# Layer 0's scores moved from its edge stage into the stage that spreads the edges

## The reference, cut to what matters

```python
h = x @ W_w + W_b                       # 6250 x 128
row, col = (edge_index[0], edge_index[1])
a_src, a_dst = (a_w[:DIM], a_w[DIM:])
e = h[row] @ a_src + h[col] @ a_dst + a_b
e = leaky_relu(e, negative_slope=0.01)
attention = softmax(e, axis=0)
msg = attention * h[col]
out = segment_sum(msg, row, num_segments=N_NODES)
```

## Time and profile before

| | |
|---|---|
| median of 3 runs | 11,844.06 us (11,843.0 to 11,853.68) |
| span of the profiled execution, first to last instruction | 10,283.7 us |
| what lies around the span (median less span) | 1,560.4 us |
| spread stage, from SP's first load to the end of GpSimd's last scatter | 520 to 2,764 us |
| edge stage of layer 0, up to the first instruction of the next stage | 2,764 to 3,785 us |

### The profile page before, as it was taken

One profiled execution on the slowest core, in us unless ns is written; L12 is line 12 of the kernel. 1 busy time (PEld: TensorE's weight loads), 2 busy tenths in 40 slices (PEclk: granted clock), 3 DMA queues, 4 the chain that ended last, 5 costly groups with the idle time before them and its releaser, 6 DMA issues. The chain is left out here.

```text
span 10283.7 us, 161996 instructions
## 1 busy us (share of the span) xinstructions
PE 6978.8 (68%) x46439; PEld 5971.3 (58%) x46440; DVE 6132.2 (60%) x14585; ACT 2692.4 (26%) x4442; POOL 5216.0 (51%) x5267
## 2 busy tenths in 40 slices
PE   3543334443377757778877763999984888888885
PEld 2243333333377655666666652666654888888885
DVE  8832222222277776666666654777776666666665
ACT  5022222222255562222222212444441000000000
POOL 0067777777500007777777752000003777777773
PEclk7766666666688878999999986999996666666665
DMA  4055454545544435555555571000002333333335
GB/s 167 13 154 156 157 157 156 157 155 158 154 122 121 120 97 158 148 149 152 152 154 152 155 124 54 0 0 0 0 1 64 104 103 106 106 104 103 104 108 82
DMA packets 1150548, 1137.43 MB, mean 111 GB/s; under 512 B 239363, under 2 KB 959825, under 8 KB 1150117
## 3 DMA queue, kind: packets, MB, share of 16 engines
q1 hardware_dynamic: 948422, 666.82, 23.0%
q0 software_dynamic: 195904, 465.66, 16.7%
q10 hardware_dynamic: 6048, 2.84, 0.1%
HBM read 731.30 MB, written 403.51 MB: 110 GB/s over the span
## 5 line engine op out<-in xcount | busy, mean ns | idle before, releaser
L1051 POOL DMA_INDIRECT buf<-node_rows,buf x1728 | 1745.0, 1010 | 527.5 <-issue 526.3
L1563 POOL DMA_INDIRECT buf<-node_rows_ln,buf x1728 | 1715.5, 993 | 563.4 <-issue 498.0
L717 POOL DMA_INDIRECT edge_rows_by_src<-buf x1728 | 1692.6, 980 | 550.8 <-issue 526.1
L1081 PE MATMUL psum<-buf 128*128 128x128 f32 x1728 | 368.9, 369 | 1306.2 <-DVE buf L1044 1306.2
L1081 PEld LDWEIGHTS psum<-buf 128*128 128x128 f32 x1728 | 300.0, 197 | 1326.6 <-issue 1326.6
L2066 PE MATMUL psum<-parts,buf 128*128 x4896 | 917.2, 329 | 99.5 <-DVE buf L2102 44.8
L809 DVE COPY buf<-buf 128x32 int32<-128x32 int32 x108 | 19.9, 185 | 1469.5 <-DMA buf<-records_by_dst 1469.3
L2044 ACT CAST buf<-psum 128x1024 bf16<-128x1024 f32 x612 | 619.2, 1012 | 693.0 <-PE psum L2055 693.0
L2082 DVE TENSOR_TENSOR buf<-buf,ends_of 128x2048 bf16<-128x2048 bf16 x616 | 727.0, 1222 | 111.5 <-issue 111.5
L2447 PE MATMUL psum<-buf 128*128 128x5 f32 x3456 | 747.9, 354 | 49.3 <-ACT buf L2424 49.3
L2447 PEld LDWEIGHTS psum<-buf 128*128 128x128 f32 x3456 | 738.3, 329 | 63.3 <-ACT buf L2424 63.3
(11 more groups left out here) (431 smaller groups left out, 14202.6 us busy)
## 6 DMA issues: line engine op xcount, KB each, us to landing
buf<-edge_rows_by_src SPq DMA_DIRECT2D x114, 1056.0 KB
buf<-edge_rows_by_src SPq DMA_DIRECT2D x110, 1024.0 KB
buf<-in_edge_attr SPq DMA_DIRECT2D x864, 128.0 KB
running_weighted_sums<-buf SPq DMA_DIRECT2D x108, 544.0 KB, 3.5
buf<-loc_rows_by_src SPq DMA_DIRECT2D x110, 512.0 KB, 5.1
buf<-loc_rows_by_dst SPq DMA_DIRECT2D x110, 512.0 KB, 4.6
running_sums<-buf SPq DMA_DIRECT2D x108, 512.0 KB
edge_rows_by_src<-buf SPq DMA_DIRECT2D x139, 260.0 KB, 2.8
```

Of the source, the lines that this page charges most:

```text
L717: nc.gpsimd.indirect_dma_start(rows, bass.IndirectOffsetOnAxis(ap=at[:, h, t:t + 1], axis=0), st[:, h, t, :], None).then_inc(scattered[h], 16)
L1051: nc.gpsimd.indirect_dma_start(rows[:, t, 0:used], None, table, bass.IndirectOffsetOnAxis(ap=stage[:, t:t + 1], axis=0)).then_inc(sem, 16)
L1081: last = nc.tensor.transpose(psT[:, sg % 2, t * P:(t + 1) * P], oh[:, 4 * sg + t, :], c["ident"][:])
L1563: nc.gpsimd.indirect_dma_start(xn[:, j, t, :], None, table1, bass.IndirectOffsetOnAxis(ap=stage[:, j // 4, at:at + 1], axis=0)).then_inc(g ...
```

## The change

The scores of layer 0 are found in the spread stage. For each half VectorE there compares two sets of one-hots in bf16 (by destination and by source, `sel`), TensorE turns both, and ScalarE copies both out of PSUM. The source's one-hots are multiplied with the three bf16 parts of the source scores of all 49 blocks at once (`find`, 48 matmuls of 49 columns), and VectorE picks each edge's own block out of the 49 columns (`of_blk`, `picked`), adds the destination's part and the bias, takes the leaky relu and writes the score into the column of the row that held the destination's part. It also keeps a maximum of the scores, which is spread to all partitions after the last half (`negm`). VectorE's order becomes: the places of half n+1, then the scores of half n. GpSimd's wait for `evacuated` goes; `placed` is now given after the score is written.

The edge stage of layer 0 goes half by half. ScalarE takes the exponent with the final maximum, VectorE makes each weighted one-hot with a single instruction per tile (compare and multiply, L1267 of the new kernel), TensorE sums and VectorE adds (L1278). Turned one-hots, the running maximum, the factor and the scaling of `agg` are gone.

```diff
             c["agg"] = agg
-            l0_edges(nc, c, ins, blk_a, a_parts, rows)
+            l0_edges(nc, c, blk_a, negm, rows)
...
                         pool.wait_ge(edge_got[h], 128 * i + 128)
-                        pool.wait_ge(evacuated, 4 * n + 6)
...
+                def keep_dst(n, g):
+                    act.wait_ge(dst_turned, 2 * n + (g + 5))
+                    act.wait_ge(expanded, 8 * n + (4 * g + 4))
+                    nc.scalar.copy(dstT[:, g, :], psT[:, 0, :]).then_inc(dst_kept, 1)
+
+                def keep_src(n, g):
+                    act.wait_ge(src_turned, 2 * n + (g + 5))
+                    act.wait_ge(scored, 2 * n + (g + 1))
+                    nc.scalar.copy(srcT[:, g, :], psT[:, 1, :]).then_inc(src_kept, 1)
+
+                def evacuate(n, h, x):
+                    act.wait_ge(expanded, 8 * n + (x + 9))
+                    nc.scalar.copy(st[:, h, 2 * x:2 * x + 2, D:D + WT], psX[:, x % 2, 0:2 * WT].rearrange("p (t k) -> p t k", t=2)).then_inc(evacuated, 1)
...
-                        evacuate(n, h, 3)
+                        keep_dst(n, 0)
+                        keep_src(n, 0)
+                        keep_dst(n, 1)
+                        for x in range(4):
+                            evacuate(n, h, x)
+                        keep_src(n, 1)
+                        for x in range(4, 8):
+                            evacuate(n, h, x)
                 for g in range(QC):
                     act.wait_ge(loc_turned, g + 1)
...
+                        def turn(w, g, turned):
+                            for t in range(G):
+                                tile = G * g + t
+                                last = nc.tensor.transpose(psT[:, w, t * P:(t + 1) * P], sel[:, h % 2, w, tile // 2, :, tile % 2], ident[:])
+                            last.then_inc(turned, 1)
+
+                        def expand(x):
+                            pe.wait_ge(evacuated, 8 * n + (x + 1))
+                            for t in range(2):
+                                tile = 2 * x + t
+                                last = nc.tensor.matmul(psX[:, x % 2, t * WT:(t + 1) * WT], dstT[:, tile // G, (tile % G) * P:(tile % G + 1) * P],
+                                                        flat(tab[:, bass.ds(blocks[x], 1), 0:WT]), start=True, stop=True)
                             last.then_inc(expanded, 1)

+                        def find(g):
+                            pe.wait_ge(src_kept, 2 * n + (g + 2))
+                            for t in range(G):
+                                for k in range(3):
+                                    last = nc.tensor.matmul(psS[:, g, t * NB:(t + 1) * NB], srcT[:, g, t * P:(t + 1) * P], parts[:, k, :], start=(k == 0), stop=(k == 2))
+                            last.then_inc(scored, 1)
...
                         pe.wait_ge(hot, n + 1)
-                        for g in range(4):
-                            pe.wait_ge(ohT_ready, 4 * n + (g + 1))
-                            turn_onehot(nc, c, oh[:, h % 2], psT, g).then_inc(turned, 1)
-                            if g:
-                                expand(g - 1)
-                        expand(3)
+                        pe.wait_ge(dst_kept, 2 * n + 1)
+                        turn(0, 0, dst_turned)
+                        pe.wait_ge(src_kept, 2 * n + 1)
+                        turn(1, 0, src_turned)
+                        pe.wait_ge(dst_kept, 2 * n + 2)
+                        turn(0, 1, dst_turned)
+                        for x in range(4):
+                            expand(x)
+                        pe.wait_ge(src_kept, 2 * n + 2)
+                        turn(1, 1, src_turned)
+                        pe.wait_ge(chosen, n + 1)
+                        find(0)
+                        pe.wait_ge(dst_kept, 2 * n + 3)
+                        for x in range(4, 8):
+                            expand(x)
+                        find(1)
...
+                    lp.link(nc.vector.tensor_scalar(locs[:, b, 0, :], place[:], -1.0, None, ALU.add))
+                    dve.wait_ge(dst_turned, 2 * n + 2)
+                    dve.wait_ge(src_turned, 2 * n + 2)
+                    for w in range(2):
+                        last = nc.vector.tensor_tensor(sel[:, b, w], bc(iota[:].unsqueeze(1), [P, PAIRS, P, 2]),
+                                                       bc(locs[:, b, w, :].rearrange("p (a t) -> p a t", t=2).unsqueeze(2), [P, PAIRS, P, 2]), ALU.is_equal)
+                    last.then_inc(hot, 1)
+                    lp.link(nc.vector.tensor_copy(node[:], field(1)))
+                    lp.link(nc.vector.tensor_tensor(key[:], node[:], field(2).bitcast(F32), ALU.subtract))
+                    lp.link(nc.vector.tensor_tensor(of_blk[:, b], blk_no[:], bc(key[:].unsqueeze(1), [P, NB, HALF]), ALU.is_equal))
+                    lp.link(nc.vector.tensor_scalar(lost[:, b], valid[:], -1.0, -NEG, ALU.add, ALU.mult))
...
+                    of_dst = st[:, h, :, SCORE:SCORE + 1].rearrange("p t o -> p (t o)")
+                    dve.wait_ge(scored, 2 * n + 4)
+                    lp.link(nc.vector.tensor_tensor(picked[:].rearrange("p (g t) k -> p g t k", g=2), psS[:, :, 0:G * NB].rearrange("p g (t k) -> p g t k", t=G),
+                                                    of_blk[:, b].rearrange("p k (g t) -> p g t k", g=2), ALU.mult))
+                    dve.sem_inc(chosen, 1)
+                    lp.link(nc.vector.tensor_reduce(score[:], picked[:], AX.X, ALU.add))
+                    dve.wait_ge(evacuated, 8 * n + 10)
+                    lp.link(nc.vector.scalar_tensor_tensor(score[:], score[:], ab[:], of_dst, ALU.add, ALU.add))
+                    lp.link(nc.vector.scalar_tensor_tensor(of_dst, score[:], 0.01, score[:], ALU.mult, ALU.max))
+                    dve.sem_inc(placed, 1)
+                    lp.link(nc.vector.tensor_tensor(cand[:], of_dst, lost[:, b], ALU.add))
+                    lp.link(nc.vector.tensor_tensor(most[:], most[:], cand[:], ALU.max))
...
+                def step(i, h):
+                    n = R * i + h
+                    if not isinstance(i, int) or n + 1 < NH:
+                        find_places(n + 1, (h + 1) % R, i if h + 1 < R else i + 1)
...
+                        find_scores(n, h, 1 if isinstance(i, int) and n == NH - 1 else 2)
...
+                dve.wait_ge(max_spread, 1)
+                nc.vector.tensor_scalar(negm, psM[:, P:P + 1], -1.0, None, ALU.mult)
...
+    agg, R = c["agg"], 4
+    assert NH % R == 0 and NT + R * HALF <= NTX
...
+                    sp.dma_start(rows[:, s], by_tile[:, s * HALF:(s + 1) * HALF, D:ROW]).then_inc(got[s], 16)
+                with sp.Fori(0, NI) as i:
+                    for s in range(R):
+                        sp.wait_ge(summed, R * i + (s + 1))
+                        sp.wait_ge(saved, R * i + (s + 1))
+                        sp.dma_start(rows[:, s], by_tile[:, bass.ds(i * (R * HALF) + (s + R) * HALF, HALF), D:ROW]).then_inc(got[s], 16)
...
+                    for s in range(R):
+                        n = R * i + s
+                        act.wait_ge(got[s], 16 * i + 16)
+                        act.wait_ge(weighed, n + 1)
+                        nc.scalar.activation(p[:, s % 2, :], rows[:, s, :, D + 1:D + 2].rearrange("p t o -> p (t o)"), ACT.Exp, bias=negm).then_inc(weights, 1)
+                        tiles = bass.ds(i * (R * HALF) + s * HALF, HALF)
...
+                    for s in range(R):
+                        n = R * i + s
+                        pe.wait_ge(weighed, n + 3)
+                        pe.wait_ge(added, PAIRS * n + 1)
+                        for q in range(PAIRS):
+                            for k in range(2):
+                                t = 2 * q + k
+                                last = nc.tensor.matmul(psA[:, s % 2, q // 3, (q % 3) * W:(q % 3) * W + D + 1], oh[:, s % 2, t, :], rows[:, s, t, 0:D + 1],
+                                                        start=(k == 0), stop=(k == 1))
+                            if q == 2:
+                                last.then_inc(partly, 1)
                         last.then_inc(summed, 1)
...
+                def weigh(n, s, i):
+                    dve.wait_ge(weights, n + 1)
+                    if not isinstance(n, int) or n >= 2:
+                        dve.wait_ge(summed, n - 1)
+                    for t in range(HALF):
+                        last = nc.vector.tensor_scalar(oh[:, s % 2, t, :], c["iota"][:], rows[:, s, t, W - 2:W - 1], p[:, s % 2, t:t + 1], ALU.is_equal, ALU.mult)
+                    last.then_inc(weighed, 1)
+
+                def add(n, s, i):
+                    blocks = pair_blocks(nc, ENG.DVE, blk, i, s, 0, R)
+                    dve.wait_ge(partly, n + 1)
...
+                        if q == 3:
+                            dve.wait_ge(summed, n + 1)
+                        dve.wait_ge(added, PAIRS * n + (PAIRS + q + 1))
```

(20 more changed lines are left out.)

378 lines of the change are left out of this document (108 added, 270 removed).

## The result

In the comparison that the prediction was made for, the changed kernel took 12,058.28 us (median of 4 runs, 12,046.06 to 12,060.26) and the kernel before, in runs made beside it, 11,848.87 (4 runs): ratio 1.0174 [1.0152, 1.0196]. The medians are 209 us apart, slower, where 168 us less were forecast.

What follows compares the result with a forecast made beforehand. Prediction: GpSimd's scatters bound the spread stage and VectorE the edge stage; -241 (edge) + 66 (contention) + 7 (start) = -168, so 11,844 - 168 = 11,676 us, range 11,580 to 11,795.

Steps and rivals of the forecast that it cites:

- 1,560.4 us lie around the span and are carried over unchanged: Whole kernel: profile span 10,283.7 us against a timed median of 11,844.06; the difference was taken as time outside the span.
- It waits for nothing else: Spread stage: GpSimd's scatters wait only for issue, so a half costs 20.6 us and 108 halves 2,220 us.
- Rival (c): Spread stage: TensorE–ScalarE hand-overs and `find` gating `placed` make a half 23.3 us, total 11,903 us, slower; chance 0.08.
- Edge stage: Edge stage of layer 0: 7.05 us a half, 761 us for 108, ending at 3,544 against 3,784.6: -241 us.
- The head: Start of the edge stage: first one-hots at 2,778.5, 16.8 us less than the 31.6 us before.
- weighted one-hot: Edge stage, VectorE: 16 in 3.23 us, 0.20 each, the lower bound; half rate would add 1.07 us for 16.
- rival (b): Edge stage half costs more: one-hots at half rate, 11,792 us, or block numbers staying dear, about 11,755; chance 0.13.
- Additions: Edge stage, VectorE: 8 additions a half stay at 3.33 us, each waiting for the one before.
- block numbers and turns: Edge stage, each half: 0.3 us for block numbers and turns between one-hots and additions, 0.2 for turns at loop ends.
- Contention: Spread stage: VectorE's two-input comparisons delay GpSimd's DMAs 0.75 us a half instead of 0.14: +66 us.
- Start: Start of the spread stage: first scatter waits for half 0's scores, about 552 instead of 545.0: +7 us.
- Sum: Whole kernel: -241 + 66 + 7 = -168 us, giving 11,676 us; chance 0.62.

Runs made afterwards that it cites:

- e1: The kernel before run again with no edit: 11,846.79 us, span 11,844.9.
- e13: The changed kernel itself, run again with no edit: 10,188.58 us, 0.9906 against the kernel before.
- e5: Kernel before with ScalarE evacuating expanded rows in 8 steps of 2 tiles instead of 4 of 4: 12,029.49 us, 0.9990.
- e4: Changed kernel with `placed` given ahead of the scores, scores written to a separate buffer, GpSimd waiting for `evacuated`: 11,976.43 us, 1.0096 against the kernel before.
- e6: Changed kernel with expansions handed over in 4 groups of 4 tiles instead of 8 of 2: 12,117.69 us, 1.0061 against the kernel before.
- e8: e4 without the source turns, their copies and `find` on TensorE and ScalarE: 11,858.94 us, 0.9849 against the kernel before.
- e9: Kernel before with 64 more narrow matmuls in each half of the spread stage: 0.9998.
- e12: e6 with only the first of three bf16 parts in `find`, 16 instead of 48 matmuls: 0.9896 against the kernel before.
- e14: Repeat of e9, 64 more narrow matmuls a half in the kernel before: 0.9997.
- e18: Repeat of e11, one fp32 matmul per tile in `find`: 0.9894 against the kernel before.
- e11: e6 with `find` made of one fp32 matmul per tile instead of three bf16 ones: 0.9898 against the kernel before.

## Why the prediction was wrong

**The step that failed is the first one**: "1,560.4 us lie around the span and are carried over unchanged". They don't lie around it. e1's span is 1,561.2 us longer than that of before, and 1,554 of it are in the three stages in which GpSimd issues indirect DMAs: 504 in the spread stage, 507 in layer 1, 543 in layer 3. The profile was of an execution of the quick kind, the three timed runs of the late kind, and there, where the forecast had -168 us, the runs showed +209. A span and a time that differ by 13%, when nothing else of the program can fill the gap, should have been read as two different conditions, and the prediction should have had a rival for it. It had none.

**"It waits for nothing else"** (a half costs 16 x 1.285 = 20.6 us "whatever the others do") was read correctly from the earlier trace rows and holds in the quick kind, where e13 keeps it. In the late kind the kernel before already waited 510 us for ScalarE's L727, so a half took 25.2 us. GpSimd there waited for TensorE's and ScalarE's chain before the change had put anything on it.

**Rival (c)**, to which I gave 0.08, comes closest to what happened in the late kind, in its sign and in its first half: `find`'s results gate `placed`, and GpSimd waits for it. Its sum of 20 hand-overs of 0.3 us is not the mechanism: e5 added four to a half at no cost. Its price was too low as well (23.3 us a half; the stage took 3,127 / 108 = 29.0). What stood in its place are increments of TensorE that come up to 20 us late in e1 and up to 36 in the changed kernel. Of the about 409 us lost in the stage (last scatter at 3,676.7 against 3,268.1), 56 are longer DMAs. By e4, 82 hang on the scores' place ahead of `placed`; by e6 134 on the two-tile groups; by e8 against e4 297 on the source part. These three compare runs of different groups, they overlap, and they are not a sum.

**The terms, in the quick kind**, where they were meant to hold:
- Edge stage, -241 forecast. From the last scatter to the next stage's first step: 2,860.4 to 3,685.0, 824.6 us, against 1,020.9 before: -196. The head was right (14.3 us to the first weighing, forecast 14.8). The mis-sized term is the weighted one-hot: 16 in 4.19 us instead of 3.23, 0.262 us each (435.5 / 1,664). I took the lower bound, 0.20, "since nothing more is streamed"; the upper bound, half the rate, gave 4.30 and was nearly right: the first half of rival (b). Additions take 3.33, as forecast, and the 0.5 us for block numbers and turns vanished. From the first weighing (2,874.7) to the end of the last addition (3,681.8) are 807 us where I had 761, so a half takes 7.47 us instead of 7.05.
- Contention, +66 forecast: GpSimd's busy time rose from 1,692.9 to 1,784.0, **+91**. The mechanism is as described: the DMA that starts at 1,504.39 lasts 2.02 us, 1.05 more than its neighbours, until 0.85 us after VectorE's two comparisons have ended. A half loses 0.99 us over 0.97 a DMA (0.062 x 16), where I took 0.75. The Trainium skill, "SBUF — State Buffer", section "Who interferes with whom", has this lock for two SBUF inputs; the runs agree, and its inference that `tensor_tensor` leaves descriptor generation alone doesn't hold here. In e13's trace 106 of the 1,728 DMAs start at least 35 ns after one of L896's comparisons has begun and more than 0.2 us before its end. Each is longer by the time from 0.13 us after its start to the comparison's end, within 10 ns: 103.5 us in all. Another 42 start 85 to 95 ns before a comparison begins, and none is longer. So the 0.13 us give the length of a wait rightly, but who began first decides whether there is one. Also, 145 start while L917 runs, one of whose inputs lies in PSUM; none is longer. e8, with one more such instruction, adds 71 ns to the mean DMA.
- Start, +7: the first scatter at 550.4 instead of 545.0, +5.
- Sum: -196 + 91 + 5 = -100, measured -97. So even there the forecast of -168 was too good by 70 us, though -97 lies inside its range (-264 to -49): there the mechanism held and two terms, the one-hots and the contention, were sized too low.

In the late kind the edge stage gained the same: from the last scatter 826.7 us against 1,027.3 in e1, -201. So the edge stage's gain is the same in both kinds; only the spread stage differs, +97 in one and +409 in the other.

**What stays open.** Why TensorE's increments are late in one kind and not in the other: the same program gave both, each kind was stable within a group, and nothing in the kernel selects it. As every group had a chip of its own, the chip, or something that was different on it at that time, is a rival that no run tests; the same kernel twice on one chip of each kind would. The times of the experiments all belong to executions with a recorded span. The Trainium skill, "NOTIFIC — the notification-queue block", section "Overflow: three behaviours, one of which stalls the engine", says that the block that writes the trace's records can be set, queue by queue, to stall the producer when a queue is full, where otherwise records are lost. That could make the engine with the most records late; no run here shows it, as none was made without records. Records are missing here too, and more of them in the late kind: 176 of TensorE's 792 in e1 against none of 783 in the profile of before, 141 of 1,209 in the changed kernel's against 24 of 1,306 in e13's. Also open is whether the number of TensorE's instructions (N) or its time (W) sets the loss: e9 to e12 and e14 to e18 all fell on the quick kind. And no version was run in the late kind that is faster than the kernel before with the scores in the rows: the nearest is e6, 1.0061, and e11's form was never run there.

## What to carry to other kernels

First set the profile's span against the timed runs. If they differ by far more than the 2 us that lay between them here, find in which stages before pricing anything; a stage that seems bound by one engine in a quick execution may be bound by a hand-over in the timed ones. Work moved "under" GpSimd's indirect DMAs cost 97 us of the stage in the quick kind and 409 in the late one, where TensorE had to hand it on; more PSUM room for TensorE to run ahead may help (e6), which isn't shown by itself. And when an instruction has one operation more than the row it is priced by, carry both bounds through the sum: here the one-hots came out at the upper one.

## What the runs showed of the hardware

- Where GpSimd issues indirect DMAs, TensorE's semaphore increments can arrive late, while ScalarE's are on time: in e1's spread stage 7 us in the median and up to 20; in the changed kernel 59% are within 0.1 us and the latest is 36 us behind. After GpSimd's last DMA of a half it takes about 2 to 3 us until they come. That happened in the spread stage of the runs at 11,850 and 12,040 us, not in those at 10,280.
- The late kind itself differs between groups: 11,853 and 12,037 us for the same kernel, with most of the difference in layer 3's gathers (2,814 us in e1, 2,947 in e5's profile, whose layer 3 is the same code).
- 64 more narrow matmuls, or 12 of 512 columns, in each half cost nothing in the quick kind (0.9996 to 0.9999).
- An indirect DMA on GpSimd that starts behind a `tensor_tensor` with two SBUF inputs waits for its end (106 DMAs of e13, 103.5 us); one that starts 85 to 95 ns ahead of it does not (42 DMAs), nor does one beside a `tensor_tensor` with an input in PSUM (145).
- VectorE's fp32 `tensor_scalar` of 128 elements from SBUF takes 0.20 us in a row of 16 with one operation and 0.26 with two operations and two scalars from SBUF.
